# Second layernorm of a fused attention and feed-forward kernel: the reciprocal deviations taken on 16 columns and spread by DMA

## The reference, cut to what matters

```
x = x + xattn(layernorm(x), ctx, ctx)      # 32 query heads, 8 key/value heads of 128, rope, tanh cap at 30, softmax, @ Wo
x = x + ffn(layernorm(x))                  # x @ W_base.T + b, plus top-2 of 8 low-rank experts of rank 16

def layernorm(x):                          # over the 1024 features of a token
    return (x - mean(x)) / sqrt(var(x) + 1e-5)
```

## Time and profile before

| | |
|---|---|
| median of 3 runs | 2150.79 us (2147.84 to 2157.55) |
| profiled execution's own time | 2149.18 us |
| its span | 2147.4 us |
| PE busy | 2129.3 us (99%) |
| PE weight loads | 1727.0 us (80%) |
| DVE busy | 1663.9 us (77%) |
| ACT busy | 882.2 us (41%) |
| POOL busy | 292.8 us (14%) |
| DMA | 237 GB/s in the mean |

### The profile page before, as it was taken

How to read it: one execution, slowest core, us unless ns; L and a number is a source line. 1 busy time by engine, 2 the same in 40 slices (tenths; PEclk the granted TensorE clock), 3 DMA queues, 4 the chain that set the end, 5 groups by cost and what they waited for, 6 DMA issues and landing times.

```text
span 2147.4 us, 26381 instructions
## 1 busy us (share of the span) xinstructions
PE 2129.3 (99%) x9429; PEld 1727.0 (80%) x9429; DVE 1663.9 (77%) x2571; ACT 882.2 (41%) x1342; POOL 292.8 (14%) x359
## 2 busy tenths in 40 slices
PE   9999999999999999998999999999999999999999
PEld 7888888888888888876778777777787777888887
DVE  6966889888887666676878789997998889857443
ACT  3323243222241111155555566655665556423221
POOL 0340001111131000013111111111112111100000
PEclk9999999999999999999999999999999999999999
DMA  8698597655596655698766786689677965696741
GB/s 327 233 343 285 212 336 275 230 212 216 215 338 230 212 202 200 235 272 271 198 197 187 225 242 181 205 271 276 193 194 218 306 187 161 212 373 263 293 183 64
DMA packets 201715, 508.50 MB, mean 237 GB/s; under 512 B 20592, under 2 KB 45808, under 8 KB 199536
## 3 DMA queue, kind: packets, MB, share of 16 engines
q1 hardware_dynamic: 181104, 443.31, 62.7%
q0 software_dynamic: 20480, 63.50, 9.3%
HBM read 357.26 MB, written 149.16 MB: 236 GB/s over the span
## 4 chain that ended last, share of the span: by engine, by line
PE 86%; DMA 7%; DVE 4%; issue 1%; ACT 1%; POOL 0%; SPq 0%; ACTq 0%; DVEq 0%; POOLq 0%
PE ps L377 28%; PE ps L379 28%; PE ps L378 28%; DMA X2D<-stg 2%; DMA RB<-rD 2%; DMA rD<-r 1%; PE ps L914 1%; DVE Rl L330 1%; DVE Y L984 1%; DMA raw<-gran 1%; DVE ps L330 1%; DMA r<-rT 1%; DVE Pl L330 0%; DVE ps L899 0%; DVE Al L330 0%
## 5 line engine op out<-in xcount | busy, mean ns | idle before, releaser
L377 PE MATMUL ps<-Ah,Rh 128*128 128x512 f32 x1024 | 399.6, 390 | 2.6 <-DVE Y L984 2.6
L379 PE MATMUL ps<-Ah,Rl 128*128 128x512 f32 x1024 | 399.2, 390 | 0.0
L378 PE MATMUL ps<-Al,Rh 128*128 128x512 f32 x1024 | 399.0, 390 | 0.0
L378 PE MATMUL ps<-Xq,qW 128*128 128x512 f32 x896 | 348.5, 389 | 0.0
L377 PE MATMUL ps<-Xq,qW 128*128 128x512 f32 x896 | 348.5, 389 | 0.0
L379 PE MATMUL ps<-Xq,qW 128*128 128x512 f32 x896 | 348.5, 389 | 0.0
L330 DVE TENSOR_TENSOR Rl<-raw,Rh 128x1024 fp32r<-128x1024 f32 x174 | 212.3, 1220 | 57.1 <-ACT Rh L326 56.7
L326 ACT ACTIVATE Rh<-raw 128x1024 fp32r<-128x1024 f32 x176 | 185.4, 1055 | 148.5 <-PE ps L379 118.0
L377 PEld LDWEIGHTS ps<-Ah,Rh 128*128 128x128 f32 x1024 | 192.5, 188 | 45.0 <-DVE Y L984 3.0
L379 PEld LDWEIGHTS ps<-Ah,Rl 128*128 128x128 f32 x1024 | 192.5, 188 | 40.5
L378 PEld LDWEIGHTS ps<-Al,Rh 128*128 128x128 f32 x1024 | 192.5, 188 | 40.1
(11 more groups left out here) (217 smaller groups left out, 3869.1 us busy)
## 6 DMA issues: line engine op xcount, KB each, us to landing
raw<-gran SPq DMA_DIRECT2D x177, 512.0 KB, 6.1
QSD<-qW SPq DMA_DIRECT2D x64, 512.0 KB, 3.0
qD<-qt SPq DMA_DIRECT2D x128, 256.0 KB, 3.2
qW<-QSD SPq DMA_DIRECT2D x64, 512.0 KB, 3.7
qf<-qD SPq DMA_DIRECT2D x64, 512.0 KB, 8.3
RB<-rD POOLq DMA_DIRECT2D x128, 256.0 KB, 7.0
qraw<-gran SPq DMA_DIRECT2D x48, 512.0 KB, 4.3
kD<-kst SPq DMA_DIRECT2D x32, 512.0 KB, 3.8
```

The lines of the kernel that those rows point to most:

```text
L377: put("pe", waits, lambda e: e.matmul(pe_out, lh, rh, start=first, stop=False, skip_group_check=more))
L378: put("pe", [], lambda e: e.matmul(pe_out, lh, rl, start=False, stop=False, skip_group_check=more))
L379: return put("pe", [], lambda e: e.matmul(pe_out, ll, rh, start=False, stop=last, skip_group_check=more), mark)
```

## The change

The reciprocal deviation is no longer worked out 128 times over on 512 columns. One partition of the scaled variance (512 values) is folded by a DMA into 32 partitions x 16 columns; Sqrt, reciprocal and the correction step work on those; a DMA stores the 512 results to a new tensor rE in memory, and a DMA reads them back to all 128 partitions of L2. All three DMAs are issued by POOL (`CHAIN`). The five DVE operations on 16 columns are given a cost of 150 in the model and are fixed to DVE (three of their forerunners were flex), and the Sqrt a cost of 2600 instead of 3100.

```diff
             def rstd():
                 b, m = ones_mm()
                 cd = cn("dve_ln")
-                v = put("dve", [m], lambda e: e.tensor_scalar(L2[:, :], ps[b][:, :], 1.0 / D, EPS, ALU.mult, ALU.add), cd)
+                v = put("dve", [m] + d_free[0], lambda e: e.tensor_scalar(L2[:, :], ps[b][:, :], 1.0 / D, EPS, ALU.mult, ALU.add), cd)
                 bank_free[b] = [v]
-                s = put("act", [v] + d_free[0], lambda e: e.activation(Dt[0][:, :], L2[:, :], ACT.Sqrt), cn("act_ln"), 3100)
-                r = put("dve", [s] + d_free[1], lambda e: e.reciprocal(Dt[1][:, :], Dt[0][:, :]), cd, 3350)
-                x = tt("flex", Dt[0][:, :], Dt[1][:, :], Dt[1][:, :], ALU.mult, [r], "ln")
-                x = tt("flex", Dt[0][:, :], Dt[0][:, :], L2[:, :], ALU.mult, [x], "ln")
-                x = put("dve", [x], lambda e: e.tensor_scalar(Dt[0][:, :], Dt[0][:, :], -0.5, 1.5, ALU.mult, ALU.add), cd)
-                rs = tt("flex", L2[:, :], Dt[0][:, :], Dt[1][:, :], ALU.mult, [x], "ln")
+                va, sq, rc, t = (Dt[i][0:32, 16 * j:16 * j + 16] for i in range(2) for j in range(2))
+
+                def small(x, fn):
+                    return put("dve", [x], fn, cd, 150)
+                x = dma(va, L2[0:1, :], [v] + d_free[0], "d_rv", 2, CHAIN)
+                s = put("act", [x], lambda e: e.activation(sq, va, ACT.Sqrt), cn("act_ln"), 2600)
+                r = put("dve", [s] + d_free[1], lambda e: e.reciprocal(rc, sq), cd, 150)
+                x = small(r, lambda e: e.tensor_tensor(t, rc, rc, ALU.mult))
+                x = small(x, lambda e: e.tensor_tensor(t, t, va, ALU.mult))
+                x = small(x, lambda e: e.tensor_scalar(t, t, -0.5, 1.5, ALU.mult, ALU.add))
+                x = small(x, lambda e: e.tensor_tensor(sq, t, rc, ALU.mult))
+                x = dma(rE[c].rearrange("(i t) -> i t", t=16), sq, [x], "d_rw", 2, CHAIN)
+                rs = dma(L2[:, :], bc(rE[c:c + 1, :], [P, T]), [x], "d_rx", 256, CHAIN)
                 d_free[0] = d_free[1] = [rs]
...
+    rE = nc.dram_tensor("rE", [C, T], F32).ap()
```

More of the change, by code:

```diff
@@ L179, in program @@
 def program(nc, xT, xN, ctxT, gran, mask, bias, cst, dram, out):
-    kD, vD, qD, XcD, QSD, X2D, x1D, rD = dram
+    kD, vD, qD, XcD, QSD, X2D, x1D, rD, rE = dram
     ctx = ExitStack()
@@ L1368 @@
     rD = nc.dram_tensor("rD", [2, 4, T], F32).ap()
+    rE = nc.dram_tensor("rE", [C, T], F32).ap()
     out = nc.dram_tensor("out", [C, P, KC, T], F32, kind="ExternalOutput").ap()
     program(nc, aps["xT"], aps["xN"], aps["ctxT"], aps["gran"], aps["mask"], aps["bias"], aps["cst"],
-            (kD, vD, qD, XcD, QSD, X2D, x1D, rD), out)
+            (kD, vD, qD, XcD, QSD, X2D, x1D, rD, rE), out)
     r = run_bass_kernel_spmd(nc, [arrays], core_ids=[0])
```

## The result

| | before | after |
|---|---|---|
| median of 20 runs | 2157.64 us (2138.53 to 2167.76) | 2163.98 us (2155.03 to 2175.55) |
| ratio, 95% interval | | 1.0049 (1.0030 to 1.0068) |
| profiled execution, span | 2147.4 us | 2160.5 us |

The changed kernel is slower, by half a per cent. The level is that of the occasion: the median of the kernel before was 2150.79 in its first three runs, 2157.64 here, and 2150.1, 2151.8 and 2152.5 beside the experiments. The two medians of 20 lie 6.3 us apart; the ratio, of runs that lie beside each other, is the number to go by: about 10.6 us.

What follows compares the result with a forecast made beforehand. PE was taken to bound the kernel. Profiled 2149.2 us, plus 0 for DVE's freed work and 0.5 for blocked queues, gave 2149.7, or 2151.3 on the median's scale, stated as 2151; range 2146 to 2160 us.

Steps and rivals of the forecast that it cites:

- The DVE work that goes: On DVE, 5.81 us per chunk removed and 1.2 added: 4.6 us gained per chunk, 18.4 us over four.
- POOL's issues: On POOL, three DMA issues added per chunk, 0.72 us for the first and 0.54 for the others, 1.8 us per chunk.
- The traffic: On the DMAs, 256 KB and two small transfers added per chunk, against 128 reads of that size already made.
- The last small operation: End of the five small DVE operations, to be done 5.15 us before the old point of the last product.
- rival A: DVE's 4.6 us more per chunk removes the small stalls and PE gets its 2.15 us: 2148.6 us; chance 0.25.
- the store 1.7 us (as rD<-r): In the new chain, storing the 512 results to rE takes 1.7 us, like the existing transfer rD<-r.
- late end: Latest L2 landing, 1381.0 us, the last small operation standing where the last product stood; blocks DVE for 4.5 us.
- a block of 4.5 us on DVE [...] costs at most 1 us: DVE standing 4.5 us at L2's first reader, or POOL 6.3 us, costs at most 1 us.
- one sample of 6.44 us: At 1495.01 us DVE had stood 6.44 us at a late RB, and PE lost 1.02 us in that stretch.
- B: POOL bounds in places, sums late, PE waits and loses clock: about 5.1 us a time; chance 0.10 three times, 0.10 once.
- D: The chain before L2 stays long since DVE queues it; counted as the late end in the forecast, no separate chance.
- signs of being wrong: New PE waits (RB, Pf, Y) over 10 us total, clock below 1.00 in new places, or r<-rT moved over 6 us.

Runs made afterwards that it cites:

- the waits gone: Changed kernel in its own order with all three transfers issued, but Sqrt not waiting for the fold nor the spread for the store; ratio to the kernel before 1.0002.
- store twice: Changed kernel in the same order, with the store made twice in a row before the spread; ratio to the kernel before 1.0115.
- the kernel on SP: Changed kernel with store, spread and fold issued by SP instead of POOL, order on ACT and DVE unchanged; ratio to the kernel before 1.0066.
- the kernel with idle transfers: Kernel before with its whole computation, plus the change's three transfers issued by POOL with nobody waiting for what they bring; ratio to the kernel before 1.0011.
- the urgent chain: Changed kernel, planner given the traced landings, and fold, Sqrt, small operations, store and spread put first on their engines; ratio to the kernel before 1.0021.
- the told kernel: Changed kernel with the planner told that fold, store and spread land 3.9, 5.9 and 5.2 us later; only order changes; ratios to the kernel before 1.0016 and 1.0008.

## Why the prediction was wrong

**What held.** PE sets the time. The DVE work that goes was put at 18.4 us and is 20.2. POOL's issues take 0.52 us each. The traffic, the three transfers with nobody waiting, is within the noise of nothing (1.0011). The last small operation comes 22.6 us after L1045 (1371.75 - 1349.14); the forecast had 22.3. And rival A's gain did not show: with the waits gone and the DVE work saved the ratio is 1.0002. Its 2.15 us, 0.1%, lie inside that interval, so what is shown is that nearly all of DVE's 20 us was hidden work, at 19.19 of 20 us too.

**The first step that failed: "the store 1.7 us (as rD<-r)".** It took 7.55 us in chunk 0. The fold took 5.8 there (put at 2.6), the spread 8.1 (7.0). L2 was there 38.9 us after L1045; I had 31.1, and 36.2 as late end. POOL stood 6.07 us, not 1.7. The 1.7 is a median over 32 transfers, most of them in moments like that at 1366, with a DMA share of 0.02. The trace of before has others in loaded moments. One is rD<-r of the group of the earlier trace rows, issued at 1480.58, its reader on POOL released at 1488.36 after a wait of 7.23 us. This is its stretch:

```profile
1480.60:1488.00 7.40, 7.40 (x34) 6.15 (x33) 5.80 (x9) 5.07 (x8) 0.53 (x1) 1.00 1.05 244
```

So the number was there to be read: not how long such a transfer takes, but how long it takes at a share of 1.05. With landings as forecast, L2 would have come 22.6 + 1.7 + 7.0 = 31.3 us after L1045; the measured store and spread made it 38.9.

**The second: "a block of 4.5 us on DVE [...] costs at most 1 us".** It rested on one sample of 6.44 us that cost 1.02. Here a block of 6.54 us made PE 4.9 us later, one of 3.83 0.6, one of 2.86 nothing. The sample had the multiplication by RB at the head of DVE, with values behind it that PE was far from; here the reader of L2 stands with only three operations between it and the mask of the scores, and the exponential and PE's reader of it follow within 4 us. The slack there is 4.26 us. The 4.5 us of the prediction's late end would, by an estimate between the lines at 4.16 and 5.41 in the table, have cost some 1.3 us, not far from its 1; what was wrong is that the sample promised the same at 6.4. Beyond 4.26 us PE waits microsecond for microsecond in chunks 0 and 1, and in the four cases with 6.48 us and more the clock falls too (0.72, 0.72, 0.50 and 0.59 over the six us behind), so PE's lateness is 1.5 to 2.4 times its wait. The ratios go the same way; by the longest wait of DVE for L2 in a trace: 3.5 and 3.6 us, 1.0005 and 1.0002 (no wait for the store); 6.54, 1.0049; 6.48, 1.0043; 9.73, 1.0115 (store twice). The kernel on SP has 5.41 and 1.0066, out of line with these; what its waits cost the loads behind them on SP was not measured. The sample was also read as idle time alone: 84 matmuls are in its 20 us against 90 at 1360, about 1.3 us of them by an estimate from these two rows. Its PE wait was 1.0 us, and the stretch behind it, in the kernel before, is whole, with 28 matmuls at full clock:

```profile
1496.00:1502.00 6.00, 4.99 (x22) 2.50 (x21) 5.45 (x9) 5.54 (x10) 0.71 (x1) 1.00 0.37 89
1502.00:1508.00 6.00, 6.00 (x28) 4.99 (x27) 6.00 (x11) 2.87 (x5) 0.75 (x2) 1.00 0.27 90
```

**The rivals.** B had the size right for one chunk (5.1 us a time forecast; 4.9, 0.6 and nothing measured) and the path wrong: its sums late behind a standing POOL did not happen. POOL stood nearly as long (5.43 us) in the kernel with idle transfers, at no cost. The case that came is D, the late end and more (38.9 us against its 36.2), which I had folded into the forecast at the wrong price.

**The level.** Between the 2150.8 us of the first three runs and 2164.0 lie 13.2 us. Of these 6.9 are the base, 2157.6 on that occasion, which nothing in the profile tells; that part of the miss was bad luck. The change's own part is 6.3 us by the two medians and 10.6 by the ratio, against a forecast of 0.5: on the base of 2150.8 it would have given 2157 to 2161, at the top of the stated range. Of the prediction's signs of being wrong, one came, a granted clock below 1.00 in a new place. The trace has 8.8: 5.5 behind the late L2, 1.6 behind Sqrt in chunk 0, the rest at places that no run ties to one of the waits. At 0.49% it lies at the edge of the half per cent that I called no change, and the interval (0.30 to 0.68%) excludes none.

**Open.** What the new order costs by itself. In all six traces in the changed order PE becomes 1.5 to 5.6 us late at the group of heads that it reaches at 1411 us in the kernel before, also with both waits gone (5.6), and in none of those with idle transfers or the urgent chain. The same six are 1.2 to 2.1 us less late at each of the two waits of 1.0 us of the kernel before, and so is the one with idle transfers, so one trace can't say what the order owes. By the timings, the told kernel was measured twice, 1.0016 and 1.0008, both with 1 in the interval; with the chain made urgent 1.0021, just without. And the load of the DMA engines was never varied alone.

## What to carry to other kernels

Price a small transfer on which something depends by transfers that ran at the same DMA share, not by the median of its shape. In a program whose order is fixed in advance a value that lands later than planned stops everything behind its first reader: ask what stands behind that reader and how soon PE needs it, and plan the real landing. In this kernel 20 us of work taken from an engine that hides behind PE bought nothing that shows, and did not pay for one new wait.

## What was not expected of the hardware

- A transfer of 2 KB took 4.3 to 7.6 us at DMA shares from 0.73 to 1.06 and 1.8 at 0.07, and one of 8 KB 1.7 us at 0.02. SP's queue was no quicker than POOL's: 7.7, 9.6 and 4.4 us for the store in chunks 0 to 2.
- One wait of PE of 2.28 us was followed by a mean granted clock of 0.72 over 6 us, part of it at the level of 1.2 GHz. The wait of 1.0 us at 1496 in the kernel before was followed by 1.00, and so was one of 1.16 us in the kernel on SP; one of 5.47 us by 0.59.
- The kernel before had medians from 2150.1 us (29 runs) to 2157.6 (20) by occasion, and single runs from 2138.5 to 2167.8, 1.4% apart; only ratios to runs beside them tell half a per cent.
